# A graph network's filter bias: added by TensorE as a bf16 product where filters are made, or by VectorE where messages are made

## The reference, cut to what matters

```python
xn = node @ Wn
f = ssp(edge @ We1 + be1)          # ssp(x) = softplus(x) - log 2
f = f @ We2 + be2
msg = xn[edge_index[1]] * f
agg = jax.ops.segment_sum(msg, edge_index[0], num_segments=N)
h = ssp(agg @ W2 + b2)
h = h @ W3 + b3
return node + h
```

## Time and profile before

| | |
|---|---|
| median of 3 runs | 5716.53 us (5711.46 to 5719.04) |
| the profiled execution | 5724.69 us |
| its span, first to last instruction | 5723.0 us |
| mean granted TensorE clock | 0.656 |
| busy: TensorE, VectorE, ScalarE, GpSimd | 2659.1, 2751.9, 1432.0, 3543.8 us |

### The profile page before, as it was taken

One profiled execution on the slowest core, in us unless ns is written; L12 is line 12 of the kernel. 1 busy time (PEld: TensorE's weight loads), 2 busy tenths in 40 slices (PEclk: granted clock), 3 DMA queues, 4 the chain that ended last, 5 costly groups with the idle time before them and its releaser, 6 DMA issues.

```text
span 5723.0 us, 55777 instructions
## 1 busy us (share of the span) xinstructions
PE 2659.1 (46%) x13337; PEld 2162.5 (38%) x13337; DVE 2751.9 (48%) x7464; ACT 1432.0 (25%) x4291; POOL 3543.8 (62%) x3833
## 2 busy tenths in 40 slices
PE   2667676666688823333333323333333223333334
PEld 2455555555466623333333313222323223233333
DVE  5688777776788823333333313333333323333333
ACT  2686565555566610000000100000000000000000
POOL 2566666566255566766666366666666566666664
PEclk8898888888777755666655655555555555555555
DMA  6566655565277721111111111111111111111111
GB/s 140 139 155 149 143 142 144 138 144 133 65 226 225 224 77 48 49 50 48 50 49 50 29 48 49 49 48 51 48 51 48 40 47 48 48 52 47 51 48 38
DMA packets 433196, 490.28 MB, mean 86 GB/s; under 512 B 88331, under 2 KB 335327, under 8 KB 432870
## 3 DMA queue, kind: packets, MB, share of 16 engines
q0 software_dynamic: 131904, 288.49, 19.4%
q1 hardware_dynamic: 296424, 194.27, 12.7%
q10 hardware_dynamic: 4542, 3.90, 0.3%
HBM read 359.63 MB, written 126.70 MB: 85 GB/s over the span
## 4 chain that ended last, share of the span: by engine, by line
another core or an unknown queue 31%; DVE 13%; issue 10%; PE 6%; DVEq 4%; ACT 0%; DMA 0%; POOL 0%; ACTq 0%; SPq 0%; POOLq 0%
DVE acc L979 10%; PE bank L1763 5%; DVEq L754 2%; DVEq L751 1%; DVE arena L1019 1%; PE bank L1700 1%; DVE stats L995 1%; DVEq L987 0%; DVE x_sb L943 0%; PE bank L1695 0%; PE bank L1742 0%; DVE moments L998 0%; DVE arena L1081 0%; DVE acc L1031 0%
## 5 line engine op out<-in xcount | busy, mean ns | idle before, releaser
L1784 POOL DMA_INDIRECT arena<-node_table,pick x1664 | 1613.8, 970 | 851.0 <-issue 482.4
L1763 PE MATMUL bank<-arena 128*128 128x128 f32 x4992 | 1145.9, 402 | 2100.3 <-DVE arena L1019 1584.0
L979 DVE TENSOR_TENSOR acc<-acc,bank 128x128 f32 x2496 | 719.0, 288 | 2437.6 <-remote 1855.3
L1763 PEld LDWEIGHTS bank<-arena 128*128 128x128 f32 x4992 | 998.1, 297 | 2263.3 <-DVE arena L1019 1693.2
L1784 POOL DMA_INDIRECT arena<-gat_table,pick x832 | 849.5, 1021 | 511.9 <-issue 221.7
L1784 POOL DMA_INDIRECT arena<-message_table,pick x832 | 808.1, 971 | 377.6 <-issue 240.6
L1019 DVE TENSOR_TENSOR arena<-iota_free,local 128x512 f32<-128x512 f32 x624 | 430.6, 690 | 0.5
L1358 ACT ACTIVATE rstd<-moments,eps_col 128x4 f32<-128x4 f32 (+2 forms) x39 | 11.6, 297 | 1600.4 <-issue 827.6
L1377 ACT COPY arena<-acc 128x128 f32 x98 | 22.1, 294 | 1479.8 <-DVE acc L979 1479.8
L1689 PE MATMUL bank<-arena 128*128 x1664 | 332.6, 362 | 41.4 <-DVE arena L1095 33.3
L1689 PEld LDWEIGHTS bank<-arena 128*128 128x128 f32 x1664 | 284.6, 258 | 109.1 <-issue 109.1
(11 more groups left out here) (263 smaller groups left out, 3640.3 us busy)
## 6 DMA issues: line engine op xcount, KB each, us to landing
message_table<-arena POOLq DMA_DIRECT2D x208, 256.0 KB, 3.3
filter_table<-arena SPq DMA_DIRECT2D x196, 256.0 KB
arena<-filter_table SPq DMA_DIRECT2D x624, 64.0 KB
xt<-edge_cols SPq DMA_DIRECT2D x131, 256.0 KB
arena<-local_rows SPq DMA_DIRECT2D x208, 128.0 KB
arena<-node_table,pick POOLq DMA_INDIRECT x1664
arena<-edge_cols SPq DMA_DIRECT2D x65, 256.0 KB
arena<-gat_table,pick POOLq DMA_INDIRECT x832
```

The source lines that it names most:

```text
L979: e.tensor_tensor(a, a, bank[6 + t % 2][:, s * P:(s + 1) * P], ALU.add).then_inc(sums, 1)
L1763: ins = e.matmul(bank[6 + n % 2][:, s * P:(s + 1) * P], hot[n % 2][:, s, :], gathered[:, slot(n, s), 0:D], start=True, stop=True)
L1784: e.indirect_dma_start(out=dst, out_offset=None, in_=table, in_offset=bass.IndirectOffsetOnAxis(ap=index, axis=0)).then_inc(done, 16)
```

## The change

`filter_row` is split into three bf16 parts (high, middle and low bits), which go to rows 0, 32 and 64 of `bias_parts`, zero elsewhere. In `f_filter` a product of `ones_b` (128x128 of ones, bf16) with `bias_parts` starts each of the four accumulations in bank 1, and the float product with We2 adds to it. The addition in the message stage is gone, and its two waits move to L1095. `half_row` is made without `out_row`. The branch for unsorted lists adds `filter_row` where it copied.

```diff
@@ set-up, VectorE
             e.memset(ones_row[:, :], 1.0).then_inc(constants, 1)
+            e.memset(ones_b[:, :], 1.0)
+            own(e.memset(bias_parts[:, :], 0.0))
...
             e.wait_ge(fold_done, 2)
-            e.tensor_tensor(filter_row[:, :], bank[4][:, 0:P], rows["L1_gnn_be2"][:, :], ALU.add)
-            q = own(e.tensor_tensor(out_row[:, :], bank[4][:, P:2 * P], rows["L1_gnn_b3"][:, :], ALU.add))
+            own(e.tensor_tensor(half_row[:, :], bank[4][:, P:2 * P], rows["L1_gnn_b3"][:, :], ALU.add))
+            q = own(e.tensor_tensor(filter_row[:, :], bank[4][:, 0:P], rows["L1_gnn_be2"][:, :], ALU.add))
             after(q)
-            e.tensor_scalar(half_row[:, :], out_row[:, :], 0.5, None, ALU.mult).then_inc(fold_taken, 1)
+            own(e.tensor_scalar(half_row[:, :], half_row[:, :], 0.5, None, ALU.mult))
+            high, mid, low = (filters[1][:, k, 0:P // 2].bitcast(BF16) for k in range(3))
+            rest = filters[1][:, 3, :]
+            t = own(e.tensor_copy(high, filter_row[:, :]))
+            after(t)
+            t = own(e.tensor_tensor(rest, filter_row[:, :], high, ALU.subtract))
+            after(t)
+            t = own(e.tensor_copy(mid, rest))
+            after(t)
+            t = own(e.tensor_tensor(low, rest, mid, ALU.subtract))
+            after(t)
+            for k, piece in enumerate((high, mid, low)):
+                ins = e.tensor_copy(bias_parts[32 * k:32 * k + 1, :], piece[32 * k:32 * k + 1, :])
+            ins.then_inc(fold_taken, 1)
@@ message stage, VectorE
                     e.wait_ge(m_spread, n + 1)
-                    after(filled[n])
+                    e.wait_ge(f_in[n % FT], f_value(n))
+                    e.wait_ge(ring[n % RT], last_filter_value(n))
...
-                n = t - 3
-                if 0 <= n < TICKS:
-                    e.wait_ge(f_in[n % FT], f_value(n))
-                    e.wait_ge(ring[n % RT], last_filter_value(n))
-                    filled[n] = own(e.tensor_tensor(filter_in[n % FT][:, :, :], filter_in[n % FT][:, :, :],
-                                                 filter_row[:, :].unsqueeze(1).to_broadcast([P, GRP, D]), ALU.add))
@@ f_filter, TensorE
                 for s in range(GRP):
+                    e.matmul(bank[1][:, s * P:(s + 1) * P], ones_b[:, :], bias_parts[:, :], start=True, stop=False)
                     ins = e.matmul(bank[1][:, s * P:(s + 1) * P], magn[u % 2][:, s * P:(s + 1) * P],
-                                   mats["L1_gnn_We2"][:, :], start=True, stop=True)
+                                   mats["L1_gnn_We2"][:, :], start=False, stop=True)
```

More of the change, by code:

```diff
@@ L226, in build_program @@
         filter_row = sb("filter_row", [P, D])
-        out_row = sb("out_row", [P, D])
         half_row = sb("half_row", [P, D])
         gcn_w = sb("gcn_w", [P, D])
+        bias_parts = sb("bias_parts", [P, D], BF16)
+        ones_b = sb("ones_b", [P, P], BF16)
         half_base = sb("half_base", [P, 1])
@@ L686, in vector @@
                     e.sem_clear(f_done)
-                    e.tensor_copy(filters[0][:, 0, :], bank[0][:, 2 * P:3 * P]).then_inc(f_made, 1)
+                    e.tensor_tensor(filters[0][:, 0, :], bank[0][:, 2 * P:3 * P], filter_row[:, :], ALU.add
+                                    ).then_inc(f_made, 1)
                 e.wait_ge(src_in, 32)
@@ L1086, in vector @@
             e.memset(degree_part[:, STEPS:SW], 0.0)
-            filled = {}
             for t in range(TICKS + 4):
```

## The result

The changed kernel took 5732.0 us (median of 20 runs, 5716.2 to 5746.9) where the kernel before took 5711.5 us (20 runs, 5696.5 to 5728.0) beside it: 1.0033 times the time, 95% interval 1.0023 to 1.0044. That is slower by some 20 us. The forecast was 5695 us, faster by 21; the value lies inside the range, the direction was wrong.

The account below looks back on a forecast made before the run. The prediction took VectorE to bound fast message ticks and TensorE slow ones, with no engine full in either stage. Message stage -35, filter stage +14 and set-up 0 gave -21 us on 5716.5, so 5695 us, range 5645 to 5735.

Parts of the forecast that it names:

- What bounds the kernel now: Message stage: VectorE sets ticks of 2.04 us at 2.4 GHz, TensorE ticks of 2.54 us at 1.2 GHz.
- Message stage, -35: Message stage: without VectorE's addition fast ticks go from 2.04 to 1.76 us, slow ones stay; 35 us saved.
- what is late next, per tick: Message stage, other engines' needs: ScalarE 1.74 us, SyncE 1.9, TensorE below 1.51 (fast) or 2.54 (slow), DMA 1.63.
- Filter stage, +14: Filter stage: four added products cost 0.28 us a unit, exposed in 50 of 196 units; 14 us longer.
- My upper bound: Filter stage: at most 0.11 us for each added product, 108 us of TensorE work in all.
- Set-up, 0: Set-up: about 1.8 us more on VectorE, covered by a wait for ScalarE's counts; 0.2, at most 2 us.
- filter rival, The filter loop pays: Filter stage: added products exposed in all units, +54 us at the lower price, 5735 us in all; chance 15%.
- three signs of being wrong: L1095 waits for a filter read, message-stage clock moves over 0.05, or filter stage grows over 30 us.
- The clock stays up: Message stage: 2.4 GHz holds, ticks near 1.9 to 2.0 us, -70 to -89 us, about 5650 us; chance 16%.
- The supply is next: Message stage: SyncE's reads or DMA stretch fast ticks to 1.9 or 2.0 us, 5715 to 5725 us; chance 20%.
- The addition is not really gone: Message stage: moved waits hold VectorE at L1095 as long as the addition did, 5730 us; chance 2%.

Follow-up runs that it names:

- a3: Changed kernel with TensorE's block-number registers loaded once in the message stage, not every fourth tick (messages wrong); 5022.2 us, 0.9907 of the kernel before.
- b1: Changed kernel with TensorE's register load moved behind the four products of the tick before; 5746.2 us, 0.9968 of the kernel before.
- d2: Kernel before, with only TensorE's register load moved behind the products; 5043.8 us, 0.9965 of the kernel before.
- e1: Changed kernel run again without an edit, on the faster kind of chip; 5040.3 us, 0.9934 of the kernel before.
- c2: Changed kernel run again without an edit, on the slower kind of chip; 5771.8 us, 1.0010 of the kernel before.

## Why the prediction was wrong

**What bounds the kernel now** was read right: two kinds of tick, VectorE at 2.04 us in the fast ones. Slow ticks stayed at 2.54 us and the share of high clock in the message stage went from 0.476 to 0.484.

**Message stage, -35: measured -12.7 and -17.7.** The step that failed is "what is late next, per tick". It counted a register load of 1.36 us every fourth tick for SyncE, and gave TensorE "at most 1.51 us", from a stretch with none. TensorE has the same load, 1.38 us in the median, between the two products of a tick. With the ticks of one fast group of four at 1.41, 1.51, 1.41 and some 3.2 us, the mean is 1.9 us, not 1.76; 114 fast ticks gain some 0.15 us each, 17 us, and not 32. With the load taken away or moved the stage got 25 and 20 us shorter (a3, b1).

ScalarE's pace was costed right, 1.74 us for a measured 1.79 us. That b1's message stage is 38 us shorter than that of before on its chip, 480.2 to 442.2 us, is not proof of the forecast's 35 us: the forecast held the clock still. With b1's clock of 0.80 its formula gives 1 / (0.60 / 1.76 + 0.40 / 2.54) + 0.05 = 2.06 us a tick, and 2.14 us were measured. The clock gave what the wait for the places, at nothing in the forecast, took. No wait for a filter read appears at L1112.

**Filter stage, +14: measured +22.5 and +26.3**, and +18.0 in b1, which has the same filter stage. The step that failed is the price, not the share that shows. A unit costs 0.47 us more where I took 0.28 (0.44 us at 2.4 GHz, where I took 0.22). In 50 units on the path that is 24 us. Of 92 us of added work 24% showed, and of 88 us in the second pair 30%; the forecast had 50 / 196, 26%. The chain that ended last, 140 to 1510 us after, runs through the filter product (6.6%), the hidden product (6.3%) and the softplus, as the forecast said, but also through the attention sums L1608 (6.4%) that the gathers wait for. My upper bound, taken from the float records of L1574, 0.11 us, was the value that came, but not by that neighbour's mechanism: it is 0.055 us for the product and 0.054 us for the change back to a float one. L1576 hid the second part, since a product of 512 columns shows none.

The Trainium skill, TensorE: Matmul & The Clock Gate, section "LDWEIGHTS (loading the stationary operand)", gives a load's time as its columns divided by 1.2 GHz, by which a load of 128 columns is estimated at 107 ns; 0.109 us was measured. But the doubled product has a load of its own too, and costs 0.055 us: the page's rule by itself does not explain the number, and the agreement with the single one is not evidence for it.

**Set-up, 0:** the first filter product starts at 148.5 us after and at 149.5 before. Nothing showed.

**The sum.** By the traces -12.7 + 22.5 - 3.9 = +5.9 us for one pair of executions, -17.7 + 26.3 - 1.3 = +7.3 for the other; the last term of each is the rest of the kernel. The medians say +20 and +8. So the sign comes from two errors of 17 to 22 and of 8 to 12 us that add up, on a difference of two near-equal terms. That 5732 us lies in the range is no merit: its upper end was the filter rival at 0.054 us a product in all units, which is not what happened. Neither was any of the three signs of being wrong met. The other 12 us of the first comparison lie between execution and median, and no trace shows where.

**The rivals.** *The filter loop pays* (15%) had the right side and place: TensorE's order, completions that come late. Its size, all units exposed, did not come. *The clock stays up* (16%) did not happen here. It did in part once the load was out of the way: 0.80 against 0.75 and 0.76. *The supply is next* (20%) did not either: SyncE waited 79.8 us for VectorE after (the two waits above without the one of 42.8 us ahead of the stage), where it had waited 64.5 us before. Once the load is gone the supply does hold TensorE up, but by the read of the places and not by the filter reads. *The addition is not really gone* (2%) did not happen.

**The chip** was no rival and should have been. On the kind without the unnamed waits the change is 0.66% faster. The 240.6 us of unnamed waits in the earlier trace rows stood in the forecast as a sign that completions are late, but not as something that may be absent elsewhere.

What stays open: why results of TensorE come late on one kind of chip; whether the filter part alone makes all of the 18 to 26 us there; how much of the gain of a3 and b1 is the pause itself and how much the clock, whose falls stand behind the loads (in d2 the load moved and the clock stayed, and 15 us were gained); and what the kernel would take with the read of the places issued earlier.

## What to carry to other kernels

When work is taken off the engine that sets the pace, list the next engines' whole streams over a full period, register loads included, not over the stretch that repeats most: a 1.1 to 2 us load every fourth tick was worth more than half of the gain. Put such a load behind the last product that others wait for. When small bf16 products are added among float ones, try one wide product in place of several short ones: 0.22 us a unit of TensorE's time in place of 0.44, though the stage's end showed it only on one kind of chip, in one trace. When the gain is the difference of two terms of one size, price each from the neighbour with the same alternation, and expect the sign to depend on the chip.

## What was not expected of the hardware

- A bf16 product of 128 columns costs 0.055 us at 2.4 GHz behind another one, and 0.109 us where a float product follows; the second record of that float product starts 0.165 us after the first instead of 0.112.
- A load of 16 registers on TensorE's queue takes 1.10 to 2.99 us (medians 1.15 to 1.66) and holds up the products behind it. The profile names another engine for the gap that it leaves.
- Two kinds of chip run the same kernel in 5711 to 5764 and in 5067 to 5070 us. On the slower, ScalarE's waits for TensorE have no releaser (274.1 us at one line of the kernel after), and VectorE's sums in the last layers wait 1784.9 us so; the granted clock of the filter stage is 0.85 there and 0.93 on the faster.
- With that load gone or moved, the changed kernel's message stage went from a granted clock of 0.75 and 0.76 to 0.80, though TensorE was busy for a smaller share of it, 84% (a3, b1) after 85 and 86% (e1, c2). 40 of the 42 falls of the clock in the kernel after, and 36 of 37 in e1, came just behind the end of a load. In the kernel before, moving the load left the clock at 0.75 (d2).
